# A fused dictionary and state-space block: batch loop unrolled, batch stages re-placed, sequence preparation 1.5 groups earlier

## What is computed

```python
x = x + _L0_conv_ref(_gn(x), negative_dict)      # nearest of 256 words by cosine, replaces a pixel if close
x = x + _L1_conv_ref(_gn(x), norm_g, ...)        # layer norm, 4 chunks of 64 channels, each a Mamba scan
...
def mamba(x, ...):                                # one sequence: 1024 steps, 128 inner channels, 16 states
    xi, z = split(x @ in_proj_w.T)
    xc = silu(causal_conv4(xi) + conv_b)
    dt, Bs, Cs = split(xc @ x_proj_w.T)
    dt = softplus(dt @ dt_proj_w.T + dt_proj_b)
    h = exp(dt * A) * h + (dt * xc) * B           # the scan over the 1024 steps
    y = sum_s(h * C) + xc * D_param
    return (y * silu(z)) @ out_proj_w.T
```

## Time and profile before

| | us |
|---|---|
| median of 3 runs | 4504.09 (4501.54 to 4519.06) |
| the profiled execution | 4512.19 |
| its span, first to last instruction | 4510.2 |
| DVE busy | 4007.9 (89%) |
| PE busy | 3849.7 (85%), mean granted clock 0.912 |
| POOL busy | 3428.0 (76%) |
| ACT busy | 2813.2 (62%) |

### The profile page before, as it was taken

How to read it: one execution, slowest core, us unless ns; L and a number is a source line. 1 busy time by engine, 2 the same in 40 slices (tenths; PEclk the granted TensorE clock), 3 DMA queues, 4 the chain that set the end, 5 groups by cost and what they waited for, 6 DMA issues and landing times. The chain is left out here.

```text
span 4510.2 us, 51449 instructions
## 1 busy us (share of the span) xinstructions
PE 3849.7 (85%) x13824; PEld 1310.1 (29%) x13840; DVE 4007.9 (89%) x3073; ACT 2813.2 (62%) x3528; POOL 3428.0 (76%) x2086
## 2 busy tenths in 40 slices
PE   3788988889898898988989888898988989889886
PEld 2222323223232322323223232232323223232221
DVE  2589998998989899898998989989898998989997
ACT  3566666666666665666666666666666656666663
POOL 2587877877778777787777778777787877878775
PEclk8899998989889898998989989898998989989998
DMA  1657576675757657576665757757577575766764
GB/s 40 154 150 193 150 196 159 180 190 140 186 149 190 185 151 189 146 189 171 175 183 139 200 149 189 191 140 192 140 191 183 157 185 150 188 166 179 191 168 113
DMA packets 217782, 752.45 MB, mean 167 GB/s; under 512 B 27400, under 2 KB 28816, under 8 KB 213392
## 3 DMA queue, kind: packets, MB, share of 16 engines
q1 hardware_dynamic: 217488, 748.91, 63.9%
HBM read 639.75 MB, written 75.50 MB: 159 GB/s over the span
## 5 line engine op out<-in xcount | busy, mean ns | idle before, releaser
L592 POOL TENSOR_TENSOR state<-state,c_all 128x1024 f32<-128x1024 f32 x1024 | 2399.8, 2360 | 291.0 <-DVE state L953 266.1
L953 DVE TENSOR_TENSOR_SCAN state<-dtb,ub 128x1024 f32<-128x1024 f32 x1024 | 2340.4, 2286 | 54.9 <-DVE ub L944 7.8
L1182 PE MATMUL ub<-u,spr 64*128 64x512 f32 x4096 | 1270.1, 684 | 380.0 <-DVE state L953 356.4
L795 ACT ACTIVATE dtb<-dtb,a_neg 128x1024 f32<-128x1024 f32 x1024 | 1159.6, 1141 | 416.4 <-DMA dtb<-dt_scratch 359.6
L944 DVE TENSOR_TENSOR ub<-ub,b_all 128x1024 f32<-128x1024 f32 x1024 | 1243.9, 1215 | 160.0 <-PE ub L1182 115.8
L1182 PEld LDWEIGHTS ub<-u,spr 64*128 64x128 f32 x4096 | 352.1, 198 | 1200.8 <-DVE state L953 771.0
L1198 PE MATMUL yp<-state,gat 128*32 128x512 f32 x4096 | 588.5, 648 | 6.1 <-POOL state L592 6.1
L1047 PE MATMUL mb<-xs,wtap 128*128 128x512 f32 x512 | 274.2, 685 | 19.7 <-DMA xs<-xn 10.6
L643 ACT ACTIVATE e_x<-mb,ncb 128x512 f32<-128x512 f32 x128 | 88.0, 687 | 242.6 <-PE mb L1047 242.6
L511 POOL TENSOR_SCALAR e_x<-e_x 128x1024 f32<-128x1024 f32 x64 | 66.5, 1040 | 214.3 <-ACT e_x L643 213.0
L668 ACT ACTIVATE dt<-mb 128x512 f32<-128x512 f32 x128 | 75.8, 592 | 236.1 <-PE mb L1078 236.1
(11 more groups left out here) (143 smaller groups left out, 4827.1 us busy)
## 6 DMA issues: line engine op xcount, KB each, us to landing
dtb<-dt_scratch SPq DMA_DIRECT2D x1024, 512.0 KB, 4.8
xs<-xn SPq DMA_DIRECT2D x128, 256.0 KB, 5.1
b_all<-bc_scratch SPq DMA_DIRECT2D x64, 512.0 KB, 6.4
c_all<-bc_scratch SPq DMA_DIRECT2D x64, 512.0 KB, 7.7
xt<-in_x SPq DMA_DIRECT2D x16, 1024.0 KB, 6.5
x_scratch<-xt SPq DMA_DIRECT2D x16, 1024.0 KB, 6.7
dt_scratch<-dt SPq DMA_DIRECT2D x64, 256.0 KB, 3.5
dt_scratch<-dt SPq DMA_DIRECT2D x128, 128.0 KB, 3.7
```

The source lines that it names most:

```text
L592: pool.tensor_tensor(v, v, c_all[:, c % 2, :], ALU.mult).then_inc(gated, 1)
L795: act.activation(dtb[:, k, :], dtb[:, k, :], ACT.Exp, scale=a_neg[:, GROUP[g]:GROUP[g] + 1]).then_inc(decayed, 1)
L953: dve.tensor_tensor_scan(state[:, g % STATES, :], dtb[:, k, :], ub[:, g % 2, :], 0.0, ALU.mult, ALU.add).then_inc(scanned, 1)
L1182: last = pe.matmul(ub[:, g % 2, h * HALF:(h + 1) * HALF], spr[lo:lo + TURN, GROUP[g] % 8, :], u[lo:lo + TURN, c % 2, h * HALF:(h + 1) * HA ...
```

## The change

The `Fori` loops go: all 16 turns are written out, so that counts waited for are constants. A turn before the last (`PENULT`) leaves out the work of an image that doesn't exist.

The group normalisation of the next image (`EARLY`: its load, `a_sum`, `a_group0`, `a_gm0`, `a_mom0`, `a_rstd0`, `a_newton0`, `a_affine0`) moves from the first sequence of its turn into the fourth sequence of the turn before, and for image 1 into the start of the program, ahead of the first group's exp on ACT and the first spread on PE. The dictionary stage (`a_sim`, `a_near`, `a_pick`, `a_hot`), which sat around the border of sequences 1 and 2, is spread over sequence 1. Its later pieces and the `c_` pieces are re-placed, mostly earlier.

The preparation of the next sequence moves up by three half-steps. `post_out` and `post_take` get one place in every sequence (12 and 13). The subtraction `prep_dd` leaves POOL and becomes `prep_dt_less` on ACT, ahead of the logarithm. The two half products `u` (from PSUM, DVE j = 24 and 25) become one over 1024 columns at j = 21 that reads the SBUF copy of dt; PE waits for it by `u_ready`.

```diff
-PE_SEQ = {5: ["prep_xc0", "prep_xc1"], 13: ["prep_raw0"], 14: ["prep_raw1"], 17: ["prep_bc"], 19: ["prep_part0"],
-          20: ["prep_dt0"], 22: ["prep_part1", "prep_dt1"], 24: ["own_z"]}
+PE_SEQ = {2: ["prep_xc0", "prep_xc1"], 10: ["prep_raw0"], 11: ["prep_raw1"], 12: ["post_out"], 14: ["prep_bc"],
+          16: ["prep_part0"], 17: ["prep_dt0"], 19: ["prep_part1", "prep_dt1"], 24: ["own_z"]}
...
-DVE_SEQ = {9: ["post_gate"], 24: ["prep_u0"], 25: ["prep_u1"]}
+DVE_SEQ = {9: ["post_gate"], 21: ["prep_u"]}
...
-            (1, 7): ["c_square1"], (1, 8): ["a_turn0"], (1, 11): ["a_turn1"], (1, 12): ["a_keep0", "a_word00"],
...
+            (0, 31): ["c_square0"], (1, 0): ["c_mean1"], (1, 1): ["c_square1"], (1, 4): ["a_turn0", "a_turn1"],
...
+EARLY = ("x_in", "a_sum00", "a_sum01", "a_group0", "a_gm0", "a_mom0", "a_rstd0", "a_newton0", "a_affine00",
+         "a_affine01")
...
-                elif name == "prep_dd":
-
-                    pool.wait_ge(dt_one, m + 1)
-                    hold_here(pool)
-                    pool.tensor_scalar(e_z[:], e_z[:], 1.0, -1.0, ALU.mult, ALU.add).then_inc(dt_less, 1)
...
                     act.wait_ge(m_full[bank], use)
-                    act.activation(dt[:, cut], mb[:, bank, :], ACT.Copy).then_inc(dt_copied, 1)
+                    act.activation(dt[:, cut], mb[:, bank, :], ACT.Copy).then_inc(m_free[bank], 1)
...
+                elif name == "prep_dt_less":
+
+                    act.wait_ge(dt_one, m + 1)
+                    act.activation(e_z[:], e_z[:], ACT.Identity, bias=minus[:, 0:1]).then_inc(dt_less, 1)
...
-                elif name.startswith("prep_u"):
-                    h = int(name[-1])
-                    cut = slice(h * HALF, (h + 1) * HALF)
-                    bank, use = banks(kind, b, (f"prep_dt{h}", c))
-                    dve.wait_ge(dt_copied, 2 * m + h + 1)
-                    dve.tensor_tensor(u[:, par, cut], mb[:, bank, :], xc[:, par, cut], ALU.mult).then_inc(m_free[bank], 1)
+                elif name == "prep_u":
+                    for h in range(2):
+                        bank, use = banks(kind, b, (f"prep_dt{h}", c))
+                        dve.wait_ge(m_free[bank], use)
+                    dve.tensor_tensor(u[:, par, :], dt[:], xc[:, par, :], ALU.mult).then_inc(u_ready, 1)
...
-            turn(FIRST, 0)
-            with pe.Fori(1, NB - 1) as b:
-                turn(LOOP, b)
-            turn(LAST, NB - 1)
+            for b in range(NB):
+                turn(kind_of(b), b)
```

More of the change, by code:

```diff
@@ L90, in plan, with kind_of @@
+EARLY = ("x_in", "a_sum00", "a_sum01", "a_group0", "a_gm0", "a_mom0", "a_rstd0", "a_newton0", "a_affine00",
+         "a_affine01")
+FIRST, LOOP, PENULT, LAST = "first", "loop", "penultimate", "last"
+def kind_of(b):
+    return {0: FIRST, NB - 2: PENULT, NB - 1: LAST}.get(b, LOOP)
 def plan(seq_plan, batch_plan, kind, c, j):
@@ L506, in do @@
                 par = (c + 1) % 2
-                t = b + 1
+                t = b + 2 if c == NC - 1 and name in EARLY else b + 1
                 if name == "prep_clamp_x":
@@ L607, in _ @@
                 do(name, "pro", -1, 0)
-            for name in ("prep_clamp_x", "prep_silu_x", "prep_dd"):
+            for name in ("prep_clamp_x", "prep_silu_x"):
                 do(name, "pro", -1, NC - 1)
-            turn(FIRST, 0)
-            with pool.Fori(1, NB - 1) as b:
-                turn(LOOP, b)
-            turn(LAST, NB - 1)
+            for name in ("a_mom0", "a_newton0"):
+                do(name, "pre", -1, NC - 1)
+            for b in range(NB):
+                turn(kind_of(b), b)
             do("c_scale0", "tail", NB, 0)
@@ L1014, in _ @@
                 do(name, "pro", -1, 0)
-            for name in ("prep_u0", "prep_u1"):
-                do(name, "pro", -1, NC - 1)
-            turn(FIRST, 0)
-            with dve.Fori(1, NB - 1) as b:
-                turn(LOOP, b)
-            turn(LAST, NB - 1)
+            do("prep_u", "pro", -1, NC - 1)
+            do("a_gm0", "pre", -1, NC - 1)
+            for b in range(NB):
+                turn(kind_of(b), b)
             for name in ("post_gate", "c_var0", "c_ctr0", "c_var1", "c_ctr1", "c_out00", "c_out01", "c_out10", "c_out11"):
@@ L1168, in do @@
                     last.then_inc(m_full[bank], 1)
-            def sequence_ready(kind, b, c):
-                for q in range(2):
-                    bank, use = banks(kind, b, (f"prep_dt{q}", c))
-                    pe.wait_ge(m_free[bank], use)
             def spread_u(b, c, g):
@@ L1243, in _ @@
                 do(name, "pro", -1, NC - 1)
-            sequence_ready("pro", -1, NC - 1)
+            do("a_group0", "pre", -1, NC - 1)
+            pe.wait_ge(u_ready, 1)
             spread_u(0, 0, 0)
-            turn(FIRST, 0)
-            with pe.Fori(1, NB - 1) as b:
-                turn(LOOP, b)
-            turn(LAST, NB - 1)
+            for b in range(NB):
+                turn(kind_of(b), b)
             for g in range(NU + 1 - BEHIND, NU, 2):
```

100 lines of the change are left out of this document (44 added, 56 removed), and 31 rows, old and new, of tables (ACT_BATCH, DVE_BATCH, PE_BATCH).

## The result

The changed kernel takes 5103.31 us (median of 4 runs, 5099.07 to 5109.42) against 4506.83 for the kernel before (4501.54 to 4519.06): ratio 1.132, 95% interval [1.1293, 1.1348]. The forecast was 4630, in a range up to 4730: slower, as said, but far more so. The profiled execution has a span of 5107.6 us, 597.4 longer than the one of before.

A forecast was written before the change was run, and what follows sets the result against it. DVE sets the end, idling 23.3 us a turn. New waits 17.4 + 11.1, plus 2 for clock, make 30.5: +7.2 x 14 = +101, with 8 + 6 + 11 +126, so 4630 us, range 4440 to 4730.

The forecast's parts named there:

- chain: Preparation from `raw` to `u` late on ACT and PE: 3.9 us a sequence, 17.4 a turn in all.
- (a): Second sequence, step 3: `prep_xc0` waits for bank 0 until `c_ctr1` frees it, the spread behind it: 2.4 us.
- (f): `a_sum11` delays the copy of dt by 0.6 us.
- clock: PE's clock adds to the new waits, and light steps come just before `xc`: +2 us a turn, bounds 0 and 6.
- (b): `a_turn0` and `a_turn1` stand together on bank 1, ACT reads the first late: spread for step 4 late by 2.3 us.
- (c): `a_word10/11`, `raw0` and `raw1` queue behind DVE's `a_mix`: 2.1 us.
- (d): `c_proj` at the late end of the chain: 1.2 us.
- (e): Third sequence: `a_var0` stands before ACT has squared the mean, 2.0 us, and `raw0` waits for `a_ctr1`, 0.5.
- Start, first and last turn: Additions outside the 14 middle turns: program start +8 us, first turn +6, last turn +11.
- That waits go and none come: Faster rival: chain in time, batch waits 5 a turn: -192 us, about 4310; with half of it 4400; chance 0.18.
- PE at half clock: Rival: half clock in `xc` and the chain of most sequences, 56 us more, 4690 to 4750; chance 0.10.
- `u` and POOL: Rival: DVE's product `u` and POOL's multiply exclude each other in SBUF: 26 us, 4656, or 151, 4780; chance 0.14.

The follow-up runs named there:

- Experiment 4: Changed kernel with PE doing each spread of u twice in groups 0, 1, 2, 4, 5, 14 and 15: 4989.74 us, ratio 1.1064.
- experiment 5: Changed kernel with the preparation's subtraction put back from ACT to POOL: 4916.79 us, ratio 1.0911.
- experiment 12: Kernel of experiment 7 with only the part from `raw` to `u` moved up by three half-steps: 4866.34 us, ratio 1.0828.
- experiment 7: Kernel before, unrolled, with batch stages re-placed as in the change but fitted to the old chain, preparation as before: 4395.57 us, ratio 0.9758.
- Experiment 10: Kernel of experiment 7 with only the convolution moved up by three half-steps: 4469.04 us, ratio 0.9937.
- experiment 1: Kernel before with its 14 loop turns written out and nothing else changed: 4432.9 us, ratio 0.9849.
- experiment 8: Changed kernel with the product `u` at half-step 25 instead of 21: 5115.82 us, ratio 1.1358.
- experiment 3: Unrolled kernel before with the preparation moved up three half-steps, subtraction on POOL, `u` in halves, three batch pieces moved up a little: 5144.4 us, ratio 1.1423.

## Why the forecast was right in direction and wrong in size

Idle of DVE in a turn, by the terms of the forecast (before: turn 5; after: turns 1 to 14):

```
                                       before   forecast   after
chain (steps 9 to 11, 4 sequences)       2.5      17.4      28.3
batch waits (a) to (f)                     -      11.1      13.0
clock                                      -       2.0   (in the others)
elsewhere                               20.8        -       16.1
sum                                     23.3      30.5      57.4
```

The miss is 26.9 us a turn. Two terms of the sum make it: the chain was mis-sized by 28.3 - 17.4 = 10.9, and the steps outside the chain and the listed bank waits, put at nothing, idle 16.1. The bank waits add 1.9, and the 2.0 that was set down for the clock is contained in the others.

**What bounds the kernel, and the loop.** DVE does set the end, and the loop's wait did go. Its worth was 68 us, not 34.8: the forecast took one engine's row for the whole. No run separates a stall for the fetch of instructions from the loop's other costs: the rows show an "issue" wait at its turns and no more. The sum counted it inside the 23.3 and so doesn't depend on it.

**The chain: the first step that failed.** Mechanism and place are as forecast, and the size was off by 11 us a turn. For the fourth sequence the forecast has `raw1` done at 6.1 after the scan; it is done at 1966.88 - 1958.17 = 8.7. Most of the difference is half clock: the spread took 2.08 and `raw0` 2.07 where 1.05 each was taken, at a granted clock of 0.50, behind a PE wait of 2.38; the D product with its sum took 3.66 for 2.91. The bank was to be free at 15.35 and was at 18.8; dt's first half took 5.4 where 3.8 was taken, behind a wait of 3.06. The wait of `u` was put at 2.0 and is 1.84. What came in addition is the wait of the scan for its exp, put at 0.3 and measured 2.23, and the spread of step 10, put at 1.6 and measured 3.02: 7.1 a sequence in place of 3.9. Experiment 4 has `raw1` read by 7.3 and dt's first matmul at 16.3, nearly as forecast, and still idles 6.3, with the first half of dt slow behind PE's wait. Without the subtraction experiments 5 and 12 idle 4.3 and 4.1 there, and run that half at or near full pace (granted clock 1.00 and 0.97). So in these rows a late ACT is paid three times: at the scan of step 9, at the multiply of step 10, and in PE's pace behind its wait. The sum has the first at 0.3, and the third only in the 2 for the clock in a whole turn.

**Less on ACT.** The forecast counted it as 1.05 of delay in the chain. It is worth 2.9 a sequence at this place, 184 us in all, a third of the whole loss (experiment 5).

**The batch stages.** (a) 2.4 at step 3 of the second sequence: 2.9. (b) 2.3 at step 4: 5.0, of which 3.7 are for the spread. (c) 2.1: 2.1. (d) and (f), 1.2 and 0.6: 0.7 together, what step 11 of the second sequence idles over the others. (e) 2.5: 2.2. Near enough in sum, though (b) was off by half. By themselves the stages' new places, in the form fitted to the old chain, are a gain (experiment 7). (a) comes with the moved convolution: that step idles nothing in experiment 7 and 2.6 in experiment 10. (b) was not taken apart: experiment 7 has nothing there, but also has `a_turn1` elsewhere. (e) is not the preparation's doing, since step 4 of the third sequence idles 2.8 in experiment 7 too.

**Elsewhere: the second step that failed, and the larger.** Outside the chain and (a) to (f) the forecast has no idle, and gives no reason. The runs have 16.1: step 3 in the other three sequences (1.7, 2.0, 2.5), where the spread stands behind a convolution that runs partly at half clock (5.08 us at 1943.92, at a granted clock of 0.72, behind a PE wait of 2.32), step 7 of the fourth (1.9), step 5 of the first (1.8), step 0 of the second (2.0), step 15 of the third (1.8). The forecast asked where a wait in the banks would arise and priced `xc` at step 2 at nothing outside the second sequence. Experiment 10 prices the convolution's move at 81 us over experiment 7. Of the steps named here two idled before: step 0 of the second sequence 5.6, step 7 of the fourth 1.0.

**Start, first and last turn.** +8 was 5.5. +6 was 38, and +11 was 36.5: the first and last turn lose as much as the others, since the preparation is in all of them. Each turn also has 2.6 of busy time more, where the forecast has slightly less.

**The rivals.** That waits go and none come: experiments 1 and 7 are it, and it holds without the preparation's move; with it no turn came near. PE at half clock (chance 0.10, 56 us): right in kind and about half in size, as the more work of experiment 4 took 115 us off; alone it leads to 4690 to 4750, not to 5103. `u` and POOL (chance 0.14, 26 us): it came about, with 25 us of DVE's time (below), but experiment 8, which takes it away, gained nothing.

**The parts together.** Over experiment 7 the change has 15.6 points: the early `raw` to `u` 10.7, the convolution 1.8, the subtraction 4.1 at that place, `u` in one piece 1.2, which is 17.8. They overlap by 2.2. Going the other way, over experiment 1, the two moves together cost 15.7 (experiment 3), 3.2 more than singly on the new batch places (10.7 and 1.8). How these overlaps divide among single waits was not taken apart, and neither was step 14 of the first sequence, which idles 7.7 in experiment 12 and 3.3 in experiment 7.

## What to carry to other kernels

To start a cross-engine chain earlier in the written order need not make its end earlier by as much: every instruction that the five orders put behind it is wanted earlier, and the end moves only by what the chain truly saves (here 1.1 of 5.2 us). Before moving it, list what will then stand between its links, and price a late link at every engine that waits behind it, not once. Price every place that the moved work takes, not only those where a known conflict arises. Where several moves come in one change, measure them apart: here, of three, the loop and the stages (in the form of experiment 7) were gains.
